# A decoder layer on one core: maxima of self-attention handled by pairs of quads, PSUM kept by single banks

## What is computed

```python
q = hidden_states @ Wq + bq            # k, v alike; rotary embedding on q and k
scores = jnp.einsum('bhqd,bhkd->bhqk', q, k) / jnp.sqrt(HD)
probs = jax.nn.softmax(scores, axis=-1)
ctx = jnp.einsum('bhqk,bhkd->bhqd', probs, v)
...
x = _layernorm(x + attn(x))
x = _layernorm(x + xattn(x, ctx_1024, ctx_1024, mask))   # logits + mask * -1e9, then a dense layer
x = _layernorm(x + relu(x @ W1 + b1) @ W2 + b2)          # 128 -> 512 -> 128
```

## Time and profile before

| | |
|---|---|
| median of 3 runs | 221.43 us (220.69 to 223.17) |
| the profiled execution's own time | 223.62 us |
| its span | 221.8 us |
| TensorE (PE) busy, products | 202.8 us, 91% |
| VectorE (DVE) busy | 173.4 us, 78% |
| ScalarE (ACT) busy | 166.1 us, 75% |
| GpSimd (POOL) busy | 93.6 us, 42% |

### The profile page before, as it was taken

The page is one execution under the profiler, slowest core; times in us unless marked ns, Lnnn a source line. Parts: engine busy times, 40 slices in busy tenths (PEclk is TensorE's granted clock), DMA queues, the critical chain, the costliest instruction groups (busy, mean ns, idle before and its releaser), DMA issues.

```text
span 221.8 us, 5032 instructions
## 1 busy us (share of the span) xinstructions
PE 202.8 (91%) x1632; PEld 152.1 (69%) x1632; DVE 173.4 (78%) x346; ACT 166.1 (75%) x248; POOL 93.6 (42%) x130
## 2 busy tenths in 40 slices
PE   7777989999898979999989998999999999999991
PEld 5555657666476546767657667776987868977991
DVE  6585998448967987848988977898788879885764
ACT  2256567778188678969998898999899997896360
POOL 9304997048085776903103600710261343221533
PEclk9996999999999999999999999999999999999998
DMA  6967639414558861743650361140230234100011
GB/s 195 400 194 219 188 86 334 115 54 159 164 173 269 206 184 36 236 145 103 192 176 5 113 192 55 56 143 1 75 92 0 99 98 112 65 3 24 23 53 47
DMA packets 21354, 28.20 MB, mean 127 GB/s; under 512 B 5424, under 2 KB 16688, under 8 KB 21328
## 3 DMA queue, kind: packets, MB, share of 16 engines
q1 hardware_dynamic: 20696, 27.08, 39.8%
q10 hardware_dynamic: 632, 0.79, 1.3%
HBM read 14.76 MB, written 11.27 MB: 117 GB/s over the span
## 4 chain that ended last, share of the span: by engine, by line
PE 66%; issue 6%; DVE 6%; ACT 5%; DMA 2%; SPq 1%; POOLq 0%; POOL 0%; ACTq 0%; DVEq 0%
PE bank L642 12%; PE scores L625 11%; PE scores L603 10%; ACT probs L1202 4%; PE bank L779 4%; PE scores L699 3%; PE bank L790 3%; PE scores L718 3%; PE scores L779 3%; PE bank L731 3%; PE scores L790 2%; DVE max_parts L1535 2%; DMA k_diag<-z_self 2%; PE bank L671 1%; PE bank L759 1%
## 5 line engine op out<-in xcount | busy, mean ns | idle before, releaser
L1535 DVE TENSOR_REDUCE max_parts<-scores 128x4 f32<-128x1024 f32 x64 | 75.7, 1217 | 18.3 <-PE scores L603 18.1
L1202 ACT ACTIVATE probs<-scores 128x1024 f32<-128x1024 f32 x64 | 63.3, 1025 | 8.0 <-PE scores L625 7.4
L603 PE MATMUL scores<-k_diag,q_rows 96*128 96x512 f32 x128 | 44.0, 434 | 6.4 <-issue 4.2
L625 PE MATMUL scores<-q_rows,k_diag 128*128 128x256 f32 x256 | 43.0, 297 | 2.3 <-ACT probs L1202 1.3
L625 PEld LDWEIGHTS scores<-q_rows,k_diag 128*128 128x128 f32 x256 | 34.5, 189 | 12.3 <-issue 7.4
L603 PEld LDWEIGHTS scores<-k_diag,q_rows 96*128 96x128 f32 x128 | 20.7, 193 | 15.5 <-issue 13.7
L1973 POOL TENSOR_TENSOR rstd<-mean_var,minus_half 128x2 f32<-128x2 f32 x23 | 15.8, 696 | 36.1 <-DVE mean_var L1569 36.0
L642 PE MATMUL bank<-probs,v_ones 128*32 128x256 f32 x512 | 30.9, 382 | 0.1
L1163 ACT COPY scores<-cross_sb 128x1024 f32<-128x1024 f32 x22 | 22.4, 1028 | 2.5 <-DVE maxx_parts L1532 2.0
L642 PEld LDWEIGHTS bank<-probs,v_ones 128*32 128x32 f32 x512 | 15.6, 109 | 11.7 <-issue 3.3
L1532 DVE TENSOR_REDUCE maxx_parts<-scores 128x16 f32<-128x1024 f32 x16 | 19.1, 1216 | 3.9 <-PE scores L699 3.9
(11 more groups left out here) (174 smaller groups left out, 358.4 us busy)
## 6 DMA issues: line engine op xcount, KB each, us to landing
z_self<-qk_parts SPq DMA_DIRECT2D x21, 256.0 KB, 2.7
q_rows<-z_self SPq DMA_DIRECT2D x8, 384.0 KB, 4.1
qx_slots<-z_qx SPq DMA_DIRECT2D x8, 384.0 KB, 3.6
k_diag<-z_self SPq DMA_DIRECT2D x30, 96.0 KB
z_qx<-qx_parts SPq DMA_DIRECT2D x8, 256.0 KB, 2.2
qk_swapped<-qk SPq DMA_DIRECT2D x12, 128.0 KB, 2.8
xT_sb<-x SPq DMA_DIRECT2D x4, 256.0 KB, 3.3
z_qx<-qx_parts SPq DMA_DIRECT2D x8, 128.0 KB, 1.7
```

The lines of the kernel that those rows point to most:

```text
L603: mm = pe.matmul(score(use, b)[:, h * S:(h + 2) * S], qr_r[0:NROWS, b % 2, g, t * P:(t + 1) * P], kd_r[0:NROWS, b % 2, h:h + 2, g, :], sta ...
L625: mm = pe.matmul(score(use, b)[:, (2 * j + kt) * S:(2 * j + kt + 1) * S], kd_r[:, b % 2, 2 * half + j, g, kt * P:(kt + 1) * P], qr_r[:, b ...
L1202: ins = nc.scalar.activation(probs[:, g, 2 * half:2 * half + 2, :, :], score(use, b), ACT.Exp, scale=KSCALE)
L1535: ins = nc.vector.tensor_reduce(max_parts[:, b % 2, 1, t, g * MROWS:g * MROWS + HQ], score(use, b).rearrange("p (h k) -> p h k", h=HQ), AX ...
```

## The change

**Pairs of quads.** max_parts, split_max, max_transposes and maxT get an argument p, the pair of quads (0 and 1, or 2 and 3). Each works on 16 rows (SROWS) instead of 32, twice a batch. The maxima of a pair are split when its own four reductions are done. maxT copies 16 rows, for two quads: 512 columns instead of 1024, into rows 96 to 111 of q_rows. exp_scores waits for the copy of its own pair and contracts 112 rows. The zeros and ones of k_diag have 16 rows, those of cross-attention keep 32 under the new name head_of_xrow.

**PSUM by banks.** The five spaces become eight banks. Scores (M, E, Xm, Y) take banks 0 and 1, 2 and 3, 4 and 5 or 6 and 7, everything else takes one bank. USES lists the uses of each bank; a score stands in the lists of both its banks and signals in the first. A use waits for the former uses of its bank or banks, one or two semaphores; 41 scores have two.

**Order and banks.** The lists of all engines and the use lists are new. TensorE's has 311 entries.

```diff
+PAIRED = 2
+SROWS = PAIRED * MROWS
...
-            for before, use in enumerate(uses.split()):
...
+        for use in USES[bank].split():
             name, b = use.split(".")
-            at[name, int(b)] = space, before
+            key = name, int(b)
+            if key not in at:
+                at[key] = bank, signals, []
+                signals += 1
+            if previous:
+                at[key][2].append(previous)
+            previous = key
...
-            return read[space], before
+            return [taken(*previous) for previous in dict.fromkeys(TURN[use, b][2])]
...
-            def max_transposes(b):
-                pe.wait_ge(max_split, b + 1)
+            def max_transposes(b, p):
+                pe.wait_ge(max_split[p], b + 1)
...
-                    mm = pe.transpose(misc("mT", b)[0:XROWS, t * P:(t + 1) * P], max_parts[:, b % 2, 0, t, :], ident)
+                    mm = pe.transpose(misc(f"mT{p}", b)[0:SROWS, t * P:(t + 1) * P], max_parts[:, b % 2, p, 0, t, :], ident)
...
             def exp_scores(b, g, half):
                 use = f"E{g}{half}"
-                pe.wait_ge(*taken("mT", b))
+                pe.wait_ge(*taken(f"mT{g // PAIRED}", b))
...
-                                       kd_r[:, b % 2, 2 * half + j, g, kt * P:(kt + 1) * P], qr_r[:, b % 2, g, :],
+                                       kd_r[0:NROWS + SROWS, b % 2, 2 * half + j, g, kt * P:(kt + 1) * P],
+                                       qr_r[0:NROWS + SROWS, b % 2, g, :],
...
-                ins = nc.scalar.copy(q_rows[max_rows, b % 2, :, :].bitcast(F32R),
-                                     misc("mT", b)[0:XROWS, 0:S].rearrange("p (o c) -> p o c", o=1).to_broadcast([XROWS, QUADS, S]))
+                ins = nc.scalar.copy(q_rows[max_rows, b % 2, 2 * p:2 * p + 2, :].bitcast(F32R),
+                                     misc(f"mT{p}", b)[0:SROWS, 0:S].rearrange("p (o c) -> p o c", o=1).to_broadcast([SROWS, PAIRED, S]))
...
-            def split_max(b):
-                for maxima in all_taken(MAXIMA, b):
+            def split_max(b, p):
+                for maxima in all_taken(MAXIMA[p], b):
```

Of the lists, the start of SP's, and of TensorE's around the first batch:

```diff
             load_wk()
+            load_rope()
             load_wq()
-            load_rope()
             load_other_xT()
+            load_xT(1)
             load_cross()
-            load_ctxT()
-            load_xT(1)
...
+            load_first_k()
             load_q(0)
-            load_first_k()
+            swap(2)
...
             kx_proj()
...
+            max_transposes(0, 0)
+            max_scores(0, 2, 1)
+            max_scores(0, 2, 0)
+            exp_scores(0, 0, 1)
+            vx_proj(1)
+            exp_scores(0, 0, 0)
             max_scores(0, 3, 0)
```

More of the change, by code:

```diff
@@ L120, in turns @@
     at = {}
-    for space, uses in USES.items():
-        for before, use in enumerate(uses.split()):
+    for bank in range(BANKS):
+        signals, previous = 0, None
+        for use in USES[bank].split():
             name, b = use.split(".")
-            at[name, int(b)] = space, before
+            key = name, int(b)
[5 more added lines that the diff above has]
+            previous = key
     return at
@@ L216, in build @@
         minus_half = sb("minus_half", [P, QT])
-        scores = psum("scores", [P, 3, 1024])
-        bank = psum("bank", [P, 2, 512])
-        written = {space: sem(f"written_{space}") for space in SPACES}
-        read = {space: sem(f"read_{space}") for space in SPACES}
-        masked = {space: sem(f"masked_{space}") for space in SPACES[:3]}
+        banks = psum("banks", [P, BANKS * BANK])
+        written, read = sems("written", BANKS), sems("read", BANKS)
+        masked = {space: sem(f"masked{space}") for space in range(0, BANKS, 2)}
         def made(use, b):
-            space, before = TURN[use, b]
+            space, before = TURN[use, b][0:2]
             return written[space], before + 1
         def taken(use, b):
-            space, before = TURN[use, b]
+            space, before = TURN[use, b][0:2]
             return read[space], before + 1
@@ L249, in earlier @@
         def earlier(use, b):
-            space, before = TURN[use, b]
-            return read[space], before
+            return [taken(*previous) for previous in dict.fromkeys(TURN[use, b][2])]
         def preset(use, b):
-            space, before = TURN[use, b]
+            space, before = TURN[use, b][0:2]
             return masked[space], 1 + sum(u[0] in "XY" for u in USES[space].split()[:before])
         def misc(use, b):
-            at = SPACES.index(TURN[use, b][0])
-            return scores[:, at, 0:512] if at < 3 else bank[:, at - 3, :]
+            at = TURN[use, b][0]
+            return banks[:, at * BANK:(at + 1) * BANK]
         def score(use, b):
-            return scores[:, SPACES.index(TURN[use, b][0]), :]
+            at = TURN[use, b][0]
+            return banks[:, at * BANK:(at + 2) * BANK]
         y_zeroed = sem("y_zeroed")
@@ L478, in _ @@
             load_k(2)
+            swap(5)
+            kx_image()
             images_low(3)
@@ new lines, in _ @@
+            pv(5, 0)
+            exp_scores(6, 0, 1)
+            maxx_scores(2, 0)
+            max_scores(6, 3, 1)
+            pv(5, 1)
+            expx_scores(1, 1)
+            expx_scores(1, 0)
+            max_scores(7, 1, 1)
+            exp_scores(6, 1, 0)
+            pv_transposes(5)
+            max_transposes(6, 1)
+            exp_scores(6, 1, 1)
+            x2_transposes(0)
+            max_scores(7, 1, 0)
+            maxx_transposes(2)
+            max_scores(7, 0, 1)
+            pvx(1)
@@ L1156, in preset_mask @@
                 act.wait_ge(mask_ready, 1)
-                act.wait_ge(*earlier(use, b))
+                for previous in earlier(use, b):
+                    act.wait_ge(*previous)
                 if use[0] == "X":
@@ new lines, in _ @@
+            first_high(1, 0)
+            warm_up()
+            qk_copy(2)
+            qk_copy(5)
+            v_copy(1)
+            v_copy(6)
+            first_high(1, 1)
+            v_copy(7)
+            qk_copy(3)
+            qk_copy(4)
+            v_copy(2)
+            diag_heads()
+            v_copy(3)
+            qk_copy(7)
+            v_copy(0)
+            maxT(0, 0)
+            exp(0, 0, 1)
+            exp(0, 0, 0)
+            v_copy(5)
+            exp(0, 1, 1)
+            maxT(0, 1)
@@ L1431, in _ @@
+            pv_copy(6, 0)
+            exp(7, 0, 0)
+            exp(7, 1, 0)
+            preset_mask("Xm0", 4)
+            pvx_copy(2)
+            x1T_copy(5)
+            exp(7, 1, 1)
+            exp(7, 0, 1)
+            maxxT(3)
+            preset_mask("Xm1", 4)
+            pv_copy(6, 1)
+            maxT(7, 1)
+            qx_copy(5)
+            expx(3, 1)
+            exp(7, 3, 1)
+            preset_mask("Y0", 3)
             att2T_copy(2)
-            relu(0, 1)
-            exp(6, 0, 1)
+            exp(7, 3, 0)
```

1188 lines of the change are left out of this document (579 added, 609 removed), and 64 rows, old and new, of the table USES.

## The result

The changed kernel takes 220.42 us (median of 20 runs, 219.0 to 222.83), the kernel before 221.78 us beside it (20 runs). The ratio is 0.9941, 95% interval 0.992 to 0.9962: 1.3 us or 0.6% faster, where 3.9 us were forecast. A second measurement, in the last but one set of experiments, gave 219.85 us and a ratio of 0.991 (0.9872 to 0.9948), 2.0 us.

The account below looks back on a forecast made before the run. TensorE was taken to set the end, losing 27.6 us to waits, mostly early. Terms -1.0 - 1.9 - 5.1 + 1.8 + 1.0 + 0 + 1.3 gave -3.9 us: 217.5 us at the median, range 212.0 to 223.0.

Parts of the forecast that it names:

- first score: Start of TensorE's scores: k loads issued ahead of q bring it to 17.1 us; gain 1.0 us, between 0 and 1.5.
- reloads: First scores of batches 2 to 7: more work covers the q and k loads; gain 1.9 us, between 0.5 and 2.6.
- spaces, with splits: PSUM score spaces: shortage 12.5 to 4.6 us at 0.65 each gains 5.1; splits and copies on busy readers cost 1.0.
- transposes: TensorE: eight more pairs of transposes of maxima, 0.22 us each, cost 1.8 us.
- order, behind 86: Late TensorE list: later cross-attention piles presets, exponents and copies on ScalarE; costs 1.3 us, between 0 and 5.
- the last one: Final step: takes the summed 3.9 us off the profiled 223.62 us and off the median 221.43 us, giving 219.7 and 217.5.
- Splits: VectorE's splits of maxima and ScalarE's copies, in halves: 4.1 us on busy readers, 1.0 on the path, between 0 and 4.7.
- rows: TensorE contracting 112 rows instead of 128: no effect.
- second waits: TensorE: 41 scores wait on two semaphores; taken as 0, at most +1.7 us.
- not the limit: Rival: score waits are a reader's queue whatever the number of spaces, no change, 222.6 us; chance 0.18.
- All pays: Rival: shortage at full price, reloads and first score at their best, splits hidden, no late pile, 211.2 us; chance 0.15.
- ScalarE takes over: Rival: in the second half 14.6 us are lost instead of 7.0, slower, 224.3 us; chance 0.15.

Follow-up runs that it names:

- c2: The changed kernel again, unchanged, one look: 220.85 us in one run.
- f4: The changed kernel again, unchanged, for a second measurement beside the kernel before: 219.85 us, ratio 0.991.
- e3: The kernel before with five products of zeros ahead of the first score, filling TensorE's idle time: 225.51 us, ratio 1.0174.
- e6: The kernel before with mask presets 64 columns wide instead of 1024 (time only): 222.32 us, ratio 1.0007.
- e2: The kernel before with PSUM kept by single banks and four score spaces, old order, no pairs: 224.86 us, ratio 1.007.
- e7: The changed kernel, order and pairs kept, with scores in only three pairs of banks; result not computed rightly: 252.59 us.
- f2: The kernel before with self-attention's reductions and exponents both halved (time only): 220.96 us, ratio 0.9897.
- g1: The kernel before with reductions and exponents halved and q and k reloads left out from batch 2 on (time only): 213.35 us, ratio 0.9594.
- e5: The changed kernel with mask presets 64 columns wide instead of 1024 (time only): 220.85 us, ratio 0.9939.
- e8: The changed kernel with self-attention's 64 reductions to maxima reading 512 of each 1024 columns (time only): 219.85 us, ratio 0.9883.
- g2: The changed kernel with self-attention's reductions and exponents both halved (time only): 220.04 us, ratio 0.9895.
- e1: The kernel before with the pairs of quads alone, old order and PSUM: 225.5 us, ratio 1.0118.
- c1: The kernel before, unchanged, measured against itself: 221.86 us, ratio 0.996.
- f3: The changed kernel with the keys' cast on ScalarE, SyncE's swap of batch 3 later and its kx_diag load of batch 4 earlier: 219.72 us.
- e10: The changed kernel with the keys' cast on ScalarE and SyncE's swap of batch 3 behind batch 1's image writes: 219.35 us, ratio 0.9869.

## Why the prediction was off

| term | forecast | measured (profile to profile) |
|---|---|---|
| first score | -1.0 | 0: 17.8, 18.2, 18.6 against 18.1, 18.2 |
| reloads | -1.9 | -2.6: slip at the first scores of batches 2 to 7, 3.65 to 1.06 (1.7 in c2, 0.0 in f4) |
| spaces, with splits | -4.1 | -5.1: what is left of the loss, and 1.2 of it is before's low clock |
| transposes | +1.8 | +1.8: the list's length by the same prices, not measured apart |
| order, behind 86 | +1.3 | +2.8 |
| sum | -3.9 | -3.4 at the last group (-0.36 for this profile's first score) |

**The step that failed is the last one:** "From its own time 219.7; at the median 217.5 us". The sum was made on a profiled execution 2.2 us above the median, and I carried the whole gain over to the median. That execution held a stretch at 0.50 behind the idle time ahead of the first score, and its 1.2 us (e3 and e6 have 4.6 and 4.7 where it has 5.8) sat in the loss that I meant to win back. Most executions don't have it. Without it the profiles differ by 2.3 us, close to the measured 1.3 and 2.0. The clock of 0.93 was in the earlier trace rows, and I read past it. The other 1.0 of the 2.2 us I can't explain.

With the 1.2 taken off, the forecast would have been 2.7 us. Two sizes did the rest, the first score and the order: together they came out 2.5 us worse than forecast, the reloads 0.7 better, and the spaces 3.9 where 2.9 would have been left to forecast. In the sum over the profiles the low clock hid that, and -3.4 for my -3.9 is in part luck.

**First score:** nothing for 1.0. The condition was right, SyncE's k issues moved from 12.98 to 11.47, but its q issue went from 12.54 to 13.20, and the first score waits for q_rows:

```profile
11.47 1.63 SPq L408 DMA_DIRECT2D k_diag<-z_self  x2
13.20 0.66 SPq L393 DMA_DIRECT2D q_rows<-z_self  x1
```

I had that as a bound ("another load ends last"), and took the gain.

**Spaces:** the amount came, 3.9 us of it without the low clock, but the reason was half right. A price for each microsecond of shortage isn't a property of the kernel: e2 took 1.3 us of shortage off and got slower, e7 added 23.6 and paid up to 1.3 for each. The lower end of its range was too high as well: with 0.15 us for each of the 51 uses 4.5 us are in excess and not 6.1, 0.36 for each us. Reloads and spaces were, as far as f2 and g1 show, not two terms to add, but two walls in series.

**Order:** 2.8 for 1.3, inside the bound of 5, but the reason was wrong: no pile on ScalarE, and not the readers' load at all (e5, e8, g2). What it is instead stays open.

**Splits, transposes, rows, second waits:** nothing speaks against them. Pairs alone cost 2.6 us for my 2.8 (e1), with an interval of 1.3 to 3.9. After's scores with two waits, from 30 on, slip no more than those with one (0.04 and 0.07 us each).

**Rivals:** "not the limit" (222.6) fails by the 8 us that after wins between positions 30 and 86 and by e7. For the order of before, though, it is half right: neither a fourth space (e2) nor readers with 54 us less to do (f2) gave it much, and its remark that pairs are little used by themselves is borne out by e1. "All pays" and "ScalarE takes over" didn't happen.

## What to carry to other kernels

Before a difference worked out on a profile goes to a median, look where that execution stands above it and why: a slice of low clock that most executions don't have can't be won at the median, and it must leave the sum first. When waits for buffers and waits for loads alternate on one engine, halve the readers' work, drop the loads, and do both, before pricing either; the first alone only brought out the other wall here. And when an order is searched anew, look at what small instructions of one-off work now lie between a split and the reduction behind it, and what GpSimd writes at that moment.

## Seen of the hardware, not expected

- A VectorE cast of 128x512 fp32 took 1.98, 2.05 and 2.44 us beside a GpSimd memset, ending 0.3 us behind it each time, and 0.43 us without one; VectorE's reductions from PSUM beside it stayed at 1.22 us, and the same cast on ScalarE at 0.62 us.
- In c1, f2 and f3 TensorE idled for 2.3, 2.7 and 2.9 us and ran at 0.50 of its clock for 3.4, 6.8 and 3.4 us, from 0.5 to 1.6 us behind the restart; idle times of 1.6 us (e6), 2.0 us (after, at 14.43) and 2.4 us (f2, at 19.27) had no such stretch behind them. In e7 no idle time near its two low stretches is above 1.5 us: from 38 to 42 us TensorE was busy for 2.84 of 4 us, in pieces. In the case of c1 the low clock cost 1.2 us on top of the wait.
- The same DMA issues land at times some 2 us apart: a wait for a DRAM write of 1.8 to 3.9 us, and rows of batch 2 late in f3 but not in e10.
